# Self-attention with four heads: key tiles taken two at a time on TensorE, the scores of both and then the value products of both

## The reference

```
def _mha_layer(q, k, v, Wq, bq, Wk, bk, Wv, bv, gamma, beta):   # q = k = v = enc, 2 x 1024 x 256, H = 4, dh = 64
    Q, K, V = relu(q @ Wq + bq), relu(k @ Wk + bk), relu(v @ Wv + bv)
    scores = einsum('hbqd,hbkd->hbqk', Qh, Kh) / sqrt(dh)
    scores = where(key_mask == 0, NEG, scores)
    attn = softmax(scores, axis=-1) * query_mask
    out = einsum('hbqk,hbkd->hbqd', attn, Vh) + q
    return _layer_norm(out, gamma, beta)
```

## Time and profile before

| | us |
|---|---|
| median of 3 runs | 1667.22 (1663.49 to 1667.71) |
| the profiled execution | 1664.12 |
| its span in the profile | 1662.4 |
| TensorE busy | 1383.4 (83%) |
| VectorE busy | 1052.6 (63%) |
| ScalarE busy | 759.0 (46%) |
| GpSimd busy | 523.9 (32%) |
| first self-attention stage, from its first scores | 751.8 to about 962 |
| second self-attention stage | 1062 to about 1273 |

### The profile page before, as it was taken

The page is one execution under the profiler, slowest core; times in us unless marked ns, Lnnn a source line. Parts: engine busy times, 40 slices in busy tenths (PEclk is TensorE's granted clock), DMA queues, the critical chain, the costliest instruction groups (busy, mean ns, idle before and its releaser), DMA issues. The chain is left out here.

```text
span 1662.4 us, 21985 instructions
## 1 busy us (share of the span) xinstructions
PE 1383.4 (83%) x7498; PEld 795.9 (48%) x7498; DVE 1052.6 (63%) x2640; ACT 759.0 (46%) x1062; POOL 523.9 (32%) x330
## 2 busy tenths in 40 slices
PE   5778999999769978788999769799997678488896
PEld 3423333333358856544444346344434566244796
DVE  5677777776355367666556467666555775675754
ACT  5304555555667444523333535233344533254664
POOL 4000000000311042206777832277785166001222
PEclk8958999999879999889999979799997889599998
DMA  6853333320000001453432107603400000830001
GB/s 231 233 124 54 55 55 55 61 49 2 26 1 1 1 1 42 136 165 89 89 78 75 45 32 214 185 21 70 90 26 26 1 1 1 185 80 3 1 1 51
DMA packets 79848, 110.31 MB, mean 66 GB/s; under 512 B 16575, under 2 KB 55673, under 8 KB 77945
## 3 DMA queue, kind: packets, MB, share of 16 engines
q1 hardware_dynamic: 79737, 108.91, 26.2%
HBM read 70.55 MB, written 37.80 MB: 65 GB/s over the span
## 5 line engine op out<-in xcount | busy, mean ns | idle before, releaser
L1239 ACT ACTIVATE x_feat<-banks,key_bias 128x1024 f32<-128x1024 f32 x160 | 176.6, 1114 | 272.1 <-PE banks L1124 210.3
L1050 POOL TENSOR_TENSOR x_feat<-x_feat 128x1024 f32<-128x1024 f32 x112 | 269.3, 2404 | 75.6 <-ACT x_feat L1239 63.7
L1082 PE MATMUL banks<-stacks 128*128 128x512 f32 (+4 forms) x640 | 229.2, 405 | 30.4 <-DVE max_parts L1265 9.1
L1139 PE MATMUL banks<-x_feat,v_group 128*64 128x512 f32 (+4 forms) x1312 | 232.4, 569 | 11.0 <-ACT x_feat L1239 10.3
L1239 ACT ACTIVATE x_feat<-banks 128x1024 f32<-128x1024 f32 (+3 forms) x224 | 179.5, 839 | 125.9 <-PE banks L1118 84.9
L1082 PEld LDWEIGHTS banks<-stacks 96*128 96x128 bf16 (+1 forms) x640 | 77.3, 138 | 200.4 <-DVE max_parts L1265 87.8
L1408 POOL TENSOR_TENSOR stacks<-w_even,stacks 128x512 fp32r<-128x512 f32 x16 | 21.9, 1401 | 470.1 <-ACT stacks L1400 470.1
L1115 PE MATMUL banks<-stacks 99*128 99x512 bf16 (+3 forms) x512 | 139.9, 347 | 12.0 <-DMA stacks<-neg_max_parts 7.4
L1265 DVE CUSTOM_DVE_ANT_0 scratch<-banks,mask_rows 128x512 f32<-128x512 f32 x128 | 88.2, 689 | 55.0 <-PE banks L1082 55.0
L1123 PE MATMUL banks<-stacks 128*128 128x512 f32 x256 | 111.2, 434 | 9.5 <-DMA stacks<-neg_max_parts_r 9.5
L1438 PE MATMUL banks<-stacks 128*128 128x512 f32 x384 | 102.9, 407 | 8.2 <-DVE stacks L1420 4.0
(11 more groups left out here) (269 smaller groups left out, 2573.7 us busy)
## 6 DMA issues: line engine op xcount, KB each, us to landing
stacks<-q_parts_r SPq DMA_DIRECT2D x18, 512.0 KB, 7.4
stacks<-k_parts_r SPq DMA_DIRECT2D x18, 512.0 KB, 10.8
q_parts_r<-stacks SPq DMA_DIRECT2D x16, 512.0 KB, 2.8
k_parts_r<-stacks SPq DMA_DIRECT2D x16, 512.0 KB, 3.6
v_group<-v SPq DMA_DIRECT2D x14, 512.0 KB, 14.6
q_parts<-y_tok SPq DMA_DIRECT2D x16, 384.0 KB, 6.1
stacks<-q_parts SPq DMA_DIRECT2D x16, 384.0 KB, 5.0
w_even<-in_w SPq DMA_DIRECT2D x4, 1024.0 KB, 6.6
```

Source lines behind the costliest of these rows:

```text
L1050: e.tensor_tensor(total, total, p, ALU.add)
L1082: m = e.matmul(PS[:, bank, at:at + wide], q[0:rows, h, qt * P:(qt + 1) * P], keys[0:rows, h, k0:k0 + wide], start=True, stop=True, skip_gr ...
L1139: m = e.matmul(PS[w * h:w * (h + 1), bank, t.q0:CH], V[:, h, :], PB[:, t.index % 2, h // 2, h % 2, 0:CH - t.q0], start=t.first, stop=t.las ...
L1239: e.activation(dst, PS[:, 2 * (st % 2):2 * (st % 2) + 2, 0:CH - t.q0], ACT.Exp, scale=A.scale, bias=bias).then_inc(s.p_ready, 1)
```

## The change

The self-attention stages get a loop of their own on TensorE. It takes tiles two at a time: the scores of both tiles, head by head, then the value product of the first and that of the second. The lists of side work of both tiles are joined, without the entries C and B, which are VectorE's; a half of the joined list is spread behind the four pieces of scores, a quarter follows each value product. The other engines' orders stay as they were, and so do all instructions.

```
+        def by_twos(i, r, work):
+            for idx in range(0, A.nt + 1, 2):
+                if idx == A.nt0 + 2 or (idx == 2 and r > 0):
+                    denominators(r - (idx == 2), int(idx == 2))
+                if A.halved and r == 0 and idx == A.nt0:
+                    e.wait_ge(s.first_rows, 2 * 16 * A.parts * A.nh)
+                two = A.tiles[idx:idx + 2]
+                chunks = [x for items in work[idx:idx + 2] for x in items if x[0] not in "CB"]
+                done = 0
+                for t in two:
+                    for h in range(2):
+                        scores(t, 0, (h,), i, r)
+                        done += 1
+                        for x in chunks[(done - 1) * len(chunks) // 8:done * len(chunks) // 8]:
+                            chunk(*x, i, r)
+                for k, t in enumerate(two):
+                    with_v(t, i, r)
+                    for x in chunks[(2 + k) * len(chunks) // 4:(3 + k) * len(chunks) // 4]:
+                        chunk(*x, i, r)
+                if not two:
+                    for x in chunks:
+                        chunk(*x, i, r)
...
+            if A.sums:
+                by_twos(i, r, work)
+                return
             for idx in range(A.nt + 1):
-                if A.sums and (idx == A.nt0 + 2 or (idx == 2 and r > 0)):
-                    denominators(r - (idx == 2), int(idx == 2))
-                if A.halved and r == 0 and idx == A.nt0:
-                    e.wait_ge(s.first_rows, 2 * 16 * A.parts * A.nh)
```

## The result

| | before | after |
|---|---|---|
| median of the runs on one chip, us | 1665.36 (4 runs) | 1681.49 (1677.04 to 1690.3, 4 runs) |
| ratio | | 1.0108 (95%: 1.0076 to 1.0139) |
| the profiled execution, us | 1664.12 | 1679.3 |
| its span, us | 1662.4 | 1677.6 |

The account below looks back on a forecast made before the run. TensorE and GpSimd were taken to share the lead, no single wait dominating. Two stages at 2.3 + 2 x 1.9 + 3.0 = 9.1 add 18 us to 1664.1, giving 1682; the median's 3.1 offset makes 1685, range 1666 to 1694.

Parts of the forecast that it names:

- Copy wait: Tiles 6 to 9: value product 8 waits for VectorE's copy of query half 0, 1.89 us instead of 0.32, +1.55.
- Transpose wait: Tiles 12 to 15: transpose of the maxima right behind the last product waits 1.68 us instead of 0.34, +1.35.
- Middle group: Second and third of a stage's four head groups: 0.5 + 0.3 - 0.3 + 1.4 = +1.9 us each.
- last piece: Tiles 12 to 15 and the next group's start in a middle group: 9.8 us becomes 11.2, +1.4.
- saving at the products: Middle group: products wait less for VectorE's maxima once spread; 1.1 us saved in tiles 6 to 9, 0.3 in 10 and 11.
- First group: Stage's first head group: same two waits, 1.3 saved at products, about 0.7 lost in its first pair; +2.3 us.
- Last group: Stage's fourth head group, without products: 0.6 + 1.9 + 0.5 = +3.0 us.
- Value product 11 ahead of the scores of tile 12: Last group, behind the denominator transposes' wait: delays exponential 12 by 1.9 us at the low clock.
- late start: Last group: GpSimd starts it 0.6 us late.
- Exponential 14: Last group: about 0.5 us late behind the norm's pieces on ScalarE.
- Stage: Each of the two self-attention stages: 2.3 + 2 x 1.9 + 3.0 = 9.1 us longer.
- clock falls too: Rival: each of 12 new waits also lowers TensorE's clock, about 3 us each, 36 in all, 1721 us; chance 0.04.

Follow-up runs that it names:

- transpose covered: Changed kernel with products of tiles 12 and 13 one behind each half of the scores, transpose of the maxima behind value product 13; ratio to before 1.0064.
- all repairs: Changed kernel with query half 0's copy first in list 8, maxima transpose behind two value products, last group's half 0 transposes a list later; ratio to before 0.9979.

## Why the prediction was right, step by step

- *Copy wait, +1.55.* Right. 1.49 us idle in six groups; 1.35 to come back when it goes; the same 1.49 in four middle groups where it is put into the kernel before.
- *Transpose wait, +1.35.* Right: 1.18 idle in six groups, 1.32 back.
- *Middle group, +1.9.* Measured +1.6 and +1.5 in the first stage, +1.7 and +1.3 in the second. The pieces were each within 0.2. (In the last piece the terms as listed add up to 11.3 and not 11.2; it measured 11.06.) The saving at the products was about 2 us a group, of which the working counted 1.4.
- *First group, +2.3.* +3.4 and +3.3. The saving of 1.3 at its products is the mis-sized term. The named waits of products for VectorE grew from 1.1 us to 2.3: 0.82 at 773.54 behind the split, then 0.55, 0.56 and 0.41 (779.23, 788.00, 795.31). Those that the timeline doesn't name (counted as for the middle groups, behind the first 5 us) fell from 3.3 to 2.1, so nothing was left of the 1.3.
- *Last group, +3.0.* +1.95 and +3.9, from other pieces than I gave. Value product 11 ahead of the scores of tile 12 was to cost 1.9, and cost nothing: from the denominator transposes to exponential 12 it is 5.40 us against 5.35. Before, the granted clock was 0.50 from 940.20 to 946.00, over value product 10, the output transposes and the scores of tile 12. Now it is 0.61 from 947.90 to 952.10, over two value products, and 1.00 behind them, so the scores run at the full clock. The late start was 0.74 where 0.6 was counted. The scores of tile 8 behind value product 7 added 0.84, a term the sum did not have. Exponential 14 cost 0.3. So exponential 12 came 1.64 us later in the group, not 2.5.
- *Stage, 9.1 each.* 8.4 and 10.25; together 18.7, forecast 18.2. That this fits so well is luck: first groups 1.0 over, middle ones 0.2 to 0.6 under, one last group 1.05 under and the other 0.9 over cancel. In the whole, two stretches outside the stages, with nothing changed in them, moved by +1.8 and -4.9 us besides. The clock's part in the second last group (0.87 instead of 0.93) is a piece of the *clock falls too* rival, some 2 us instead of 36.
- *What is hidden.* The forecast counted the key loads as a fixed 12.65 us from the group's start. In the kernels read the first product behind such a wait began 12.1 to 14.1 us after it, so a saving in a middle group could vanish in it, as it did in one of four in *transpose covered*.

## What to carry to other kernels

Two orders written by hand must be moved together. TensorE gained about 2 us a middle group by pairing, as its products waited less for VectorE. More than that was lost, because VectorE's copy and the end of the product list kept places that fitted the old order. Before regrouping an engine's queue, list each instruction that waits for another engine and how much work lies between its producer's last input and it; work enough there was worth 1.2 to 1.5 us a wait. A spacing that is longer than the work can hide a wait for which the profile names no idle time. And look for waits nobody needs yet ahead of work that feeds the bounding chain: moving half 0's transposes one list on gave 3.7 to 5.0 us a stage, in either order, about half of what the change had cost a stage.

## What the runs showed of the hardware

The first group of a stage came in two lengths in the tile-by-tile order, 54.6 to 54.9 and 58.4 to 58.5 us (with the two waits put in, 56.9 and 60.6). It was the long one in 4 of the 10 such groups that were profiled, in four kernels. What differs is when VectorE's last instruction of the split, with two inputs in SBUF and 16x128 elements, starts against the sum on GpSimd. In the kernel before, second stage, VectorE and GpSimd:

```profile
1080.73 0.28 DVE L1302 TENSOR_TENSOR neg_max_parts_r<-neg_max,neg_max_parts_r 16x128 fp32r<-16x128 f32 x1 [0.45 <-issue]
```

```profile
1080.77 2.46 POOL L1050 TENSOR_TENSOR x_feat<-x_feat 128x1024 f32<-128x1024 f32 x1 [0.18 <-issue]
```

And in the kernel with the middle groups paired, first stage: VectorE, GpSimd, and the product on TensorE that waits for the next maximum:

```profile
770.60 2.49 DVE L1332 TENSOR_TENSOR neg_max_parts_r<-neg_max,neg_max_parts_r 16x128 fp32r<-16x128 f32 x1
```

```profile
770.59 2.36 POOL L1050 TENSOR_TENSOR x_feat<-x_feat 128x1024 f32<-128x1024 f32 x1 [0.18 <-issue]
```

```profile
773.75 0.50 PE L1082 MATMUL banks<-stacks 128*128 128x512 f32 x1 [2.36 <-DVE max_parts L1295]
```

0.04 us ahead of the sum it takes 0.28 us; 0.01 us behind it, 2.49, until the sum is over. Behind the wait of 2.36 us the windows view has a granted clock of 0.60 (773.70 to 776.00) and 0.80 (to 780), and together that is 3.7 us. The Trainium skill (SBUF — State Buffer, section SBUF: two separate sides) says that such an instruction and one of GpSimd that reads SBUF take a shared pair of ports for their whole duration, whoever starts first; the trace agrees, with VectorE's end 0.14 us behind the sum's. In the paired order the split begins about 1.1 us into a sum and lasts 1.0 to 1.4: all 16 paired first groups show the same wait of 0.8 and none the long one. So with all repairs pairs cost the first group 1 us against a lucky one and save 2.7 against an unlucky one. Whether the order can be made to meet the gap each time was not tried.

The same meeting lies behind the 4.41 us for which the denominator transposes wait in the last group. In the kernel before, ahead of VectorE's copy of the denominators, and in a stretch without sums:

```profile
934.68 2.22 DVE L413 SCALAR_TENSOR_TENSOR minus_mean_rstd<-mean_var,rstd 128x4 f32<-128x4 f32 x1
937.31 2.12 DVE L413 SCALAR_TENSOR_TENSOR minus_mean_rstd<-mean_var,rstd 128x4 f32<-128x4 f32 x1
...
974.17 0.16 DVE L413 SCALAR_TENSOR_TENSOR minus_mean_rstd<-mean_var,rstd 128x4 f32<-128x4 f32 x1
```

The sums run from 934.52 to 936.89 and from 937.06 to 939.41, and the two instructions end with them (936.90 and 939.43). So some 4 of the 4.41 us are this norm instruction, two inputs of 128x4 elements, standing behind sums, and not work of VectorE. What the last group gains if it doesn't meet them was not tried.
